# Group 2's low parts and the last splits behind the early list, and the last group's first root from ScalarE

## The reference

```
x = layernorm(x + attention(x))          # 16 heads of 64, causal, biases
x = layernorm(x + cross_attention(x, ctx))   # each query sees one key: v @ Wout
x = layernorm(x + ffn(x))
ffn(x) = sum over the best 2 of 8 experts of weight * (silu(x @ up + b) @ down + b)
         + silu(x @ sh_up + b) @ sh_down + b      # the shared expert
layernorm(x) = (x - mean) / sqrt(var + 1e-5)
```

## Time and profile before

| what | us |
|---|---|
| median of three runs | 459.45 |
| the three runs | 458.13 to 461.33 |
| the profiled execution, its own time | 459.26 |
| its span, first to last instruction | 457.5 |
| PE busy in the span | 438.9 (96%) |
| DVE, ACT, POOL busy | 307.1, 300.6, 211.2 |

### The profile page before, as it was taken

One profiled execution on the slowest core, in us unless ns is written; L12 is line 12 of the kernel. 1 busy time (PEld: TensorE's weight loads), 2 busy tenths in 40 slices (PEclk: granted clock), 3 DMA queues, 4 the chain that ended last, 5 costly groups with the idle time before them and its releaser, 6 DMA issues.

```text
span 457.5 us, 11055 instructions
## 1 busy us (share of the span) xinstructions
PE 438.9 (96%) x3657; PEld 396.5 (87%) x3657; DVE 307.1 (67%) x1243; ACT 300.6 (66%) x927; POOL 211.2 (46%) x246
## 2 busy tenths in 40 slices
PE   8999999999999999999999999997989999999981
PEld 7889898988989889898998988996888999999961
DVE  3376676778786766688675869699686725333485
ACT  3688656676766766668676566856464686776535
POOL 1899598440205011210156564288503587566521
PEclk9999999999999999999999999999799999999997
DMA  5950121400300001020011314022202654343675
GB/s 156 322 183 0 63 93 46 142 0 1 122 20 0 2 13 36 25 71 0 1 48 48 93 59 126 1 71 81 83 1 79 176 165 148 117 129 121 207 256 203
DMA packets 26543, 40.16 MB, mean 88 GB/s; under 512 B 3199, under 2 KB 17683, under 8 KB 26483
## 3 DMA queue, kind: packets, MB, share of 16 engines
q1 hardware_dynamic: 21532, 27.86, 19.7%
q0 software_dynamic: 3408, 9.33, 5.7%
q10 hardware_dynamic: 1547, 2.27, 1.7%
HBM read 26.83 MB, written 12.61 MB: 86 GB/s over the span
## 4 chain that ended last, share of the span: by engine, by line
PE 83%; DVE 8%; DMA 3%; ACT 2%; issue 1%; SPq 1%; POOL 1%; ACTq 0%; POOLq 0%
PE bank L310 17%; PE bank L311 17%; PE bank L312 17%; PE bank L824 7%; PE bank L874 7%; PE bank L835 7%; DMA ex_raw<-y_dram 3%; PE bank L1041 2%; PE bank L1017 2%; PE bank L775 2%; PE bank L919 1%; PE bank L752 1%; PE bank L1027 1%; DVE probs L1489 1%; PE bank L909 1%
## 5 line engine op out<-in xcount | busy, mean ns | idle before, releaser
L1204 ACT ACTIVATE probs<-probs,negmax 128x128 f32<-128x128 f32 x256 | 99.7, 393 | 24.5 <-DVE negmax L1478 24.5
L1478 DVE CUSTOM_DVE_ANT_0 probs<-bank,mask 128x128 f32<-128x128 f32 x256 | 62.3, 285 | 45.4 <-PE bank L824 45.4
L310 PE MATMUL bank<-w_hi,ot_hi 128*128 (+1 forms) x284 | 80.9, 285 | 0.0
L311 PE MATMUL bank<-w_lo,ot_hi 128*128 (+1 forms) x284 | 80.6, 284 | 0.0
L312 PE MATMUL bank<-w_hi,ot_lo 128*128 (+1 forms) x284 | 80.4, 283 | 0.0
L310 PE MATMUL bank<-xt_hi,w_hi 128*128 128x512 f32 (+1 forms) x148 | 60.0, 405 | 0.0
L1489 DVE TENSOR_TENSOR probs<-probs,rsum 128x512 f32<-128x512 f32 x64 | 58.3, 912 | 2.2
L311 PE MATMUL bank<-xt_lo,w_hi 128*128 128x512 f32 (+1 forms) x148 | 58.0, 392 | 0.0
L312 PE MATMUL bank<-xt_hi,w_lo 128*128 128x512 f32 (+1 forms) x148 | 58.0, 392 | 0.0
L611 POOL DMA_INDIRECT xg_dram<-xacc,place x32 | 33.5, 1047 | 52.2 <-PE bank L835 29.6
L1216 ACT ACTIVATE ot_hi<-bank,cols 128x512 fp32r<-128x512 f32 x32 | 22.0, 686 | 51.8 <-PE bank L874 51.8
(11 more groups left out here) (247 smaller groups left out, 1062.1 us busy)
## 6 DMA issues: line engine op xcount, KB each, us to landing
qkv<-xg_dram SPq DMA_DIRECT2D x39, 128.5 KB, 2.1
ex_raw<-in_w_experts SPq DMA_DIRECT2D x18, 256.0 KB, 2.7
w_raw<-in_w_quads SPq DMA_DIRECT2D x10, 256.0 KB, 4.6
xacc<-in_x SPq DMA_DIRECT2D x4, 512.0 KB, 4.5
ex_raw<-in_w_cross SPq DMA_DIRECT2D x4, 512.0 KB, 3.9
w_raw<-in_ctx_t_in ACTq DMA_DIRECT2D x4, 512.0 KB, 3.8
w_raw<-in_w_quads SPq DMA_DIRECT2D x3, 512.0 KB, 6.3
xacc<-in_x_t SPq DMA_DIRECT2D x3, 512.0 KB, 6.4
```

Of the source, the lines that this page charges most:

```text
L310: pe.matmul(o, a_hi, b_hi, start=first, stop=False)
L311: pe.matmul(o, a_hi, b_lo, start=False, stop=False)
L1204: nc.scalar.activation(tile, tile, ACT.Exp, scale=-1.0, bias=negmax[:, s.par, h, j:j + 1], accum_out=sums[:, s.par, h, j:j + 1]).then_inc( ...
L1478: nc.vector.tensor_tensor_reduce(probs[:, s.par, h, slices(j, P)], sc_bank[h][:, slices(j, P)], mask[:, :], -SCALE, 3.0e38, ALU.add, ALU.m ...
```

## The change

POOL waits for `lists_ready` instead of `probs_ready` ahead of `x2_lo(2)`, and spreads what followed: two sends, a wait for all of `o_added`, split 16, two sends, a wait for `hid_ready` (the low parts of the shared hidden layers), split 17. PE waits for all splits behind the first two tile turns instead of ahead of the shared product. On DVE the counts and the early list become one sequence, `list_early`, in slot 32: three steps ahead of `take_o_lo`, the rest behind it. What only the later list needs moves to `list_between`, run behind the shared additions. The first root of the last group is made as the second was: ACT takes the square root behind `var1_ready`, DVE inverts and refines it (`last_root`). For that ACT loads the Sqrt table behind `shared_hidden(0)`, and the Silu table again behind the root.

```diff
                 split_expert(i)
             for c in range(GT):
                 send(2, c)
-            pool.wait_ge(probs_ready, 2 * SLOTS)
+            pool.wait_ge(lists_ready, 1)
             x2_lo(2)
-            for c in range(GT, 2 * GT):
+            for c in range(GT, GT + 2):
                 send(2, c)
+            pool.wait_ge(o_added, 2 * UNITS)
             split_expert(16)
+            for c in range(GT + 2, 2 * GT):
+                send(2, c)
+            pool.wait_ge(hid_ready, 2 * G - 2)
             split_expert(17)
             for i in range(AHEAD):
                 target_of(i)
...
                     pe.wait_ge(x2_split_last, 2)
                     pe.wait_ge(place_ready, G)
-                    pe.wait_ge(count_taken, 2)
+                    pe.wait_ge(count_taken, 1)
...
             load_numbers(0)
             x2_turn(G - 1, 0)
             x2_turn(G - 1, 1)
-            pe.wait_ge(ex_split, len(STAGED))
...
             tile_turn_x(0)
             tile_turn_x(1)
+            pe.wait_ge(ex_split, len(STAGED))
             for i in range(TILES + 2):
                 if i < TILES:
...
             shared_hidden(0)
+            nc.scalar.activation(warm[:, :], eps_col[:, :], ACT.Sqrt).then_inc(table_ready, 1)
+            act.wait_ge(var1_ready, 1)
+            nc.scalar.activation(root_of[:, 0, :], mv[:, 0, :, 1], ACT.Sqrt, bias=eps_col[:, :]).then_inc(root1_ready, 1)
+            act.wait_ge(table_ready, 2)
+            nc.scalar.activation(warm[:, :], eps_col[:, :], ACT.Silu).then_inc(table_ready, 1)
             shared_hidden(1)
             shared_hidden(2)
+            act.wait_ge(table_ready, 3)
             nc.scalar.activation(warm[:, :], eps_col[:, :], ACT.Sqrt).then_inc(table_ready, 1)
             act.wait_ge(var2_ready, 1)
             nc.scalar.activation(root_of[:, 1, :], mv[:, 1, :, 1], ACT.Sqrt, bias=eps_col[:, :]).then_inc(root2_ready, 1)
-            act.wait_ge(table_ready, 2)
+            act.wait_ge(table_ready, 4)
             nc.scalar.activation(warm[:, :], eps_col[:, :], ACT.Silu)
             norm2_half()
...
                 if s.p == SLOTS - 2:
                     drip(parts, 3)
-                if s.p >= SLOTS:
-                    flush(parts)
+                if s.p == SLOTS:
+                    drip(parts, 3)
                 o_lo_first = s.p >= SLOTS - 2
                 if s.evac_o and o_lo_first:
                     take_o_lo()
...
                 dve.wait_ge(o_added, 2 * QUADS * (g + 1))
-                moments(0, g)
+                moments(0, g, var1_ready if g == G - 1 else None)
...
-            def last_root2():
-
-                v, r, q = var_eps[:, 1, :], rstd[:, 1, :], root_sq[:, 1, :]
-                dve.wait_ge(var2_ready, 1)
-                nc.vector.tensor_scalar(v, mv[:, 1, :, 1], EPS, None, ALU.add)
-                dve.wait_ge(root2_ready, 1)
-                step(nc.vector.reciprocal(r, root_of[:, 1, :]))
+            def last_root(which, var_done, root_done):
+
+                v, r, q = var_eps[:, which, :], rstd[:, which, :], root_sq[:, which, :]
+                dve.wait_ge(var_done, 1)
+                nc.vector.tensor_scalar(v, mv[:, which, :, 1], EPS, None, ALU.add)
+                dve.wait_ge(root_done, 1)
+                step(nc.vector.reciprocal(r, root_of[:, which, :]))
                 step(nc.vector.tensor_tensor(q, r, r, ALU.mult))
                 step(nc.vector.scalar_tensor_tensor(out=q, in0=q, scalar=-0.5, in1=v, op0=ALU.mult, op1=ALU.mult))
                 step(nc.vector.scalar_tensor_tensor(out=r, in0=q, scalar=1.5, in1=r, op0=ALU.add, op1=ALU.mult))
...
-            def list_counts():
+            def list_early():
 
                 counts = fr_bank[:, GT * NE:GT * NE + NE]
                 f = need[:, :]
                 dve.wait_ge(rank_done, G - 1)
                 nc.vector.memset(start[:, 2 * NE:2 * NE + 1], 0.0)
                 yield from tiles_in(counts, -(P / 2 - 0.5), f)
-                yield from tiles_in(counts, P / 2 - 0.5, top[:, 0:NE])
-                nc.vector.tensor_scalar(count[:, 3, :], f, -1.0, None, ALU.mult).then_inc(count_taken, 1)
-
-            def list_early():
-
-                f, a = need[:, :], whole[:, :]
-                dve.wait_ge(count_taken, 1)
+                nc.vector.tensor_scalar(count[:, 0, :], counts, P / 2 - 0.5, 1.0 / P, ALU.add, ALU.mult)
+                nc.vector.tensor_scalar(count[:, 3, :], f, -1.0, None, ALU.mult)
                 at = issue(nc.vector.tensor_tensor(summed, upto[:, 0:NE, 0:NE],
                                                    f.unsqueeze(1).to_broadcast([P, NE, NE]), ALU.mult))
...
                 nc.vector.scalar_tensor_tensor(out=list_row[:, 0:EARLY], in0=target_f[:, 0:EARLY], scalar=float(P),
                                                in1=tile_base[:, 0:EARLY], op0=ALU.mult, op1=ALU.add
                                                ).then_inc(lists_ready, 1)
-                left = count[:, 2, :]
-                at = issue(nc.vector.tensor_tensor(left, f, ends[:, 0:NE], ALU.subtract))
-                yield
-                dve.wait_ge(dve_step, at)
+                yield
+
+            def list_between():
+
+                f, a, s, left = need[:, :], whole[:, :], count[:, 1, :], count[:, 2, :]
+                nc.vector.tensor_tensor(left, f, ends[:, 0:NE], ALU.subtract)
+                at = issue(nc.vector.tensor_scalar(s, count[:, 0, :], ROUND, None, ALU.add))
+                yield
+                dve.wait_ge(dve_step, at)
+                nc.vector.tensor_scalar(top[:, 0:NE], s, -ROUND, None, ALU.add)
                 at = issue(nc.vector.tensor_scalar(left, left, float(EARLY), 0.0, ALU.add, ALU.max))
                 yield
...
             small[SLOTS - 1] = lambda: itertools.chain(places(G - 2), shift_logits(most))
-            small[SLOTS] = list_counts
-            small[SLOTS + 1] = list_early
+            small[SLOTS] = list_early
             inside.setdefault(SLOTS + 1, []).append(lambda: hidden_lo(0))
             all_slots(lambda s: slot(s, inside, small), behind)
             stats1(G - 1)
-            flush(root(0))
+            last_root(0, var1_ready, root1_ready)
             add_cross(G - 1, 0)
             add_cross(G - 1, 1)
             hidden_lo(1)
             stats2(G - 1)
-            last_root2()
+            last_root(1, var2_ready, root2_ready)
             norm2_half()
             hidden_lo(2)
             add_shared(0)
             add_shared(1)
+            flush(list_between())
             parts = best_two(G - 1)
```

More of the change, by code:

```diff
@@ L278, in decoder_program @@
         shift2_ready, x2_half = sem("shift2_ready"), sem("x2_half")
+        var1_ready, root1_ready = sem("var1_ready"), sem("root1_ready")
         var2_ready, root2_ready = sem("var2_ready"), sem("root2_ready")
```

## The result

The changed kernel takes 456.81 us (median of 17 runs, 455.04 to 458.32) where the kernel before, on the same chip, takes 459.45 (17 runs, 457.80 to 461.81): ratio 0.9942, interval 0.9929 to 0.9956, 2.64 us faster. The forecast was 454.8, its range 453.4 to 458.3. The profiled execution takes 455.83 us, 454.1 of it the span, against 459.26 and 457.5.

What follows compares the result with a forecast made beforehand. The prediction took PE as the bound, so only its waits or lower clock give time. 5.41 us gained less 0.93 given back is 4.48, from 459.26 to 454.78 profiled; forecast 454.8 us, range 453.4 to 458.3.

Steps and rivals of the forecast that it cites:

- Part 1: Slot 32 to the last group's first variance: moving the third low parts behind the early list gains 5.4 us.
- rival (b): Low parts on POOL hold the last slot's low part on DVE: 457.0, or 459.5 with the clock down; 8%.
- rival (c): L1697's stall isn't the low parts' doing and stays: 460.4, up to 463.4 with the clock down; 7%.
- PE's idle 2.85 us and the fall of the clock go: Behind slot 32: about 3 us of PE idleness and up to 3 more from half clock over 6 us vanish.
- Part 2: POOL's respread sends and last splits, and PE's later wait for splits: covered by other work, no cost.
- Part 3: First variance to the last group's turn: the first root from ACT makes 10.75 us of 9.82, 0.93 us given back.
- rival (a): PE's lower clock moves to its 2.1 us idleness ahead of the turn: price 2 us, 456.8; 28%.

Runs made afterwards that it cites:

- e9: e1 with POOL's old order behind the low parts (sends 4 to 7 in one run, then splits 16 and 17, without the two new waits): 458.46 us.
- e5: Kernel before with one line changed, POOL waiting for lists_ready instead of probs_ready ahead of the third low parts: 461.09 us, ratio 1.0027.
- b2: The kernel before, run again unchanged for a second trace: 459.01 us.
- e2: Kernel before with only the last group's first root moved to ACT, with its two table loads: 460.41 us, ratio 1.0035.
- e1: Changed kernel with the first root made by Newton steps on DVE again, the rest of the change kept: 455.22 us, ratio 0.9919.
- e12: Kernel before with eleven added matmuls, result unused, where PE waits behind the stall: 459.03 us, ratio 0.9995.
- e13: e1 run once more, unchanged: 455.92 us, ratio 0.9916.
- e11: Changed kernel with eight added matmuls, result unused, ahead of the last group's turn: 456.35 us, ratio 0.9938.

## Why the prediction was right in its path and wrong in its size

**Part 1, the changed kernel's side: right to 0.1 us.** From the value product of slot 32 the prediction puts the low part's end 2.6 us later, the last value product 3.35 and V1 11.81 (315.2, 315.94 and 324.4, less 312.59). Measured: 2.60, 3.44, 11.89. The low part took its 0.75 beside POOL, so rival (b) is refuted; L1708 took 0.17, so rival (c) is too. The 0.2 us that the prediction charged for `hidden_lo(0)` beside the low parts wasn't needed: it waits for ACT until 321.64, and the low parts end at 321.58. The Trainium skill, SBUF — State Buffer, section Who interferes with whom, which the prediction weighed, is borne out: the low part with an input in PSUM passed POOL untouched, the steps with both inputs in SBUF (1.15 us in e9, 1.20 in e5) did not. The instruction that the change is about, L1697, isn't of that kind: it has one input, in SBUF. Such one-input steps waited too, 3.23 us in b2 and 1.29 and 1.31 in e5.

**Part 1, the kernel before's side: the mis-sized term.** "PE's idle 2.85 us and the fall of the clock go" is what failed. Of the 5.41 us booked for part 1, 3.0 are the stall itself (last value product 6.36 behind slot 32's, then 3.35) and 2.4 lie behind it, mostly the fall. The first half holds: 6.36 to 3.44, 2.92 us. Of the second only 0.96 us is there in b2, where the clock held: from the last value product to V1 are 9.41 us in b2 and 8.45 in the changed kernel. So part 1 brings 3.9 us where the clock holds, and 5.3 against the one trace in which it fell. I took the fall as a property of the kernel, and it is one of some executions: the same idleness was followed by it once (2.85 us, the first trace) and not the two other times (2.83 in b2, 2.84 in e2). I also didn't ask what would be late next *in the kernel before* with PE at its upper clock. That is the second low part and `hidden_lo(0)`, and they take back about half of what the clock gives.

The last two columns of the table show that b2 is the right base. Measured from it, the trace of every kernel comes within 0.75 us of its median's difference; from the first trace of before, the change would be 4.63 us faster and e1 5.12, and no median says so. e12 says it in its own way: with the idleness filled, no change can be told.

**Part 2, costed at nothing: right, because of its waits.** Split 16 held only one small step of DVE (L1644, 0.40 us at 326.15, 0.23 more than its other run); SP's first tile load went at 331.59, and PE waited for neither. `list_between` takes 1.06 us where DVE waits for the route product, and 0.65 us of that wait are left: nothing, as booked. e9 shows the price that the prediction didn't name: 3.0 us with these instructions in their old order, since POOL starts later and V1 comes earlier, which puts both splits on the root.

**Part 3: direction right, 0.93 booked, 0.70 to 0.76 in the traces.** V1 to turn is 10.53 us (9.83 and, in b2, 9.77 before); the prediction has 10.75. ACT's second root starts 7.65 us behind V1, not 7.85. But DVE's second variance comes 6.6 us behind V1 (332.73), not 5.8: its low part at 329.67 waits 0.69 us for ACT's high part, which is queued behind the root and the Silu load. That delay is hidden, since DVE still waits 1.18 us at the second root; ACT's chain alone sets the turn, as predicted. e1 and e2 agree that the kernel is better off without part 3, by 1.1 to 1.2 us (e1, e13) and 1.1 us (e2) in the medians, more than the traces show (0.5 and 0.8). The rest would fit rival (a): PE idles 1.86 to 2.10 us ahead of the turn with part 3, and 1.16 to 1.51 without it in the kernel before, e1, e5 and e12; and e2 has the group of executions with low mean clocks, which take 2.8 us longer than its others (in the kernel before, the like group takes 0.5 us longer). No trace of e2 or of the changed kernel shows a fall there, so this is argued, not shown.

**Rival (a)** has the nearest number, 456.8, by another road. In the changed kernel's trace the clock holds at the turn, and keeping PE busy there (e11) brings no gain that can be told. Three of the changed kernel's 17 executions have a mean clock of 0.991 or less and average 457.85 us, the other 14 average 456.33; that makes 0.3 us of the mean. That the measured time lies inside the stated range is luck as far as the mechanism goes: the range reaches to 458.3 for this rival's sake, and the forecast's own sum of 4.48 us was 1.8 too large. **The sum** in the traces is 2.92 + 0.96 - 0.76 = 3.12 us, as in the table; the median says 2.64, with an interval of 2.0 to 3.3. What is left, 0.5 us, lies inside that interval and stays open: the stretch from the turn to the end alone differs by 1.5 us between single traces.

## What to carry to other kernels

A fall of the clock in one trace is not yet a term of a sum: look at a second execution of the same kernel before it is booked, and ask what is late next once PE runs at full speed. When a wait is moved to end a collision, follow what now lies beside the moved work to its last instruction; e5 and e9 each move the same work into another chain and lose all or most of the gain. A root on ACT that needs two table loads is cheap for DVE only if nothing that DVE needs stands behind these loads in ACT's order.

## What the hardware showed that I had not expected

How long PE idles in one place doesn't decide the granted clock alone: it went to half behind 2.85 us in one execution of the kernel before, stayed at 1.00 behind 2.83 in another and behind 2.84 in e2, and fell behind 2.90 in e5 (0.50 over 3 us) and behind only 2.42 in e9 (0.57 over 4 us). Small steps pay a whole POOL subtraction each: four elements a partition took 1.15 us instead of 0.16 twice in one root (e9), and an eight-element step took 3.23 us beside two subtractions back to back, though it began ahead of their record (b2).
